# A router and expert kernel: the first 17 expert tiles wait for the rows of three groups instead of four, and VectorE's work around group 0 and the bias table stands elsewhere

## What is computed

```python
a = jax.nn.softmax(e, axis=-1)                   # 32 keys around each token
v = jnp.einsum('bts,bsf->btf', a, x)
...
probs = jax.nn.softmax(xt @ Wr + br, axis=-1)
top_p, top_idx = jax.lax.top_k(probs, TOP_K)
weights = top_p / top_p.sum(axis=-1, keepdims=True)
xe = xn[None, :, :] * ln_g[:, None, :] + ln_b[:, None, :]
h = jax.nn.gelu(jnp.einsum('end,edh->enh', xe, W1) + b1[:, None, :], approximate=False)
y = jnp.einsum('enh,ehd->end', h, W2) + b2[:, None, :]
out = (weights[:, :, None] * sel).sum(axis=1)    # sel: the rows of y of the two chosen experts
```

## Time and profile before

| | before |
|---|---|
| median of three runs | 971.86 us (970.84 to 972.05) |
| the profiled execution | 972.06 us, span 970.2 us |
| mean granted TensorE clock | 0.940 |
| TensorE, VectorE busy | 811.6 us (84%), 722.1 us (74%) |
| ScalarE, GpSimd busy | 618.1 us (64%), 608.7 us (63%) |
| routing stage | about 696 to 808 us |
| tile stream | about 811 to 936 us |

### The profile page before, as it was taken

How to read it: one execution, slowest core, us unless ns; L and a number is a source line. 1 busy time by engine, 2 the same in 40 slices (tenths; PEclk the granted TensorE clock), 3 DMA queues, 4 the chain that set the end, 5 groups by cost and what they waited for, 6 DMA issues and landing times. The chain is left out here.

```text
span 970.2 us, 25223 instructions
## 1 busy us (share of the span) xinstructions
PE 811.6 (84%) x8069; PEld 506.3 (52%) x8069; DVE 722.1 (74%) x1846; ACT 618.1 (64%) x1384; POOL 608.7 (63%) x758
## 2 busy tenths in 40 slices
PE   2888999999999999999999989847677746999950
PEld 2455555555555555555555544411355524999940
DVE  4586888888888888888888853669788651777747
ACT  4577777777878777787777832248534503888830
POOL 1127887878878788787888839810007772666650
PEclk8899999999999999999999999967999867999985
DMA  7007999994000000000000033032001111333327
GB/s 235 1 2 148 157 207 158 65 6 2 0 0 0 0 0 0 0 0 0 0 0 0 0 90 87 0 104 90 3 4 54 49 53 53 83 90 92 93 67 237
DMA packets 105406, 54.10 MB, mean 56 GB/s; under 512 B 42624, under 2 KB 96664, under 8 KB 105360
## 3 DMA queue, kind: packets, MB, share of 16 engines
q1 hardware_dynamic: 98976, 43.34, 28.9%
q0 software_dynamic: 4544, 9.38, 3.0%
q10 hardware_dynamic: 1840, 0.79, 0.4%
HBM read 21.49 MB, written 29.44 MB: 52 GB/s over the span
## 5 line engine op out<-in xcount | busy, mean ns | idle before, releaser
L398 POOL TENSOR_TENSOR s_w<-s_xsh,s_w_mem 128x512 f32<-128x512 f32 x186 | 251.8, 1354 | 8.9 <-DVE s_w_mem L570 3.4
L570 DVE SCALAR_TENSOR_TENSOR s_w_mem<-s_w_mem,s_eta,lp_g 128x256 f32<-128x256 f32 x496 | 217.8, 475 | 24.0 <-PE lp_g L733 18.6
L495 ACT ACTIVATE s_xsh<-s_w,l_keep_lr 128x256 f32<-128x256 f32 x384 | 173.8, 505 | 17.5 <-POOL l_keep_lr L418 17.4
L1484 POOL DMA_INDIRECT f_yg<-f_yr,f_xmeta x78 | 78.4, 1005 | 54.5 <-DVE f_yr L1823 41.7
L1479 POOL DMA_INDIRECT f_xg<-f_xrow,f_place x64 | 64.0, 999 | 48.0 <-DVE f_place L1719 28.8
L403 POOL TENSOR_TENSOR s_xsh<-s_w,l_keep 128x512 f32<-128x512 f32 x64 | 72.1, 1126 | 0.0
L1459 ACT ACTIVATE f_hh<-fp_v,f_bcol 128x256 f32<-128x256 f32 x156 | 61.1, 476 | 13.1 <-DVE f_hs_lo L1814 5.6
L489 ACT COPY l_wt<-lp_b 128x512 f32<-128x512 f32 x96 | 56.4, 588 | 15.0 <-PE lp_b L719 15.0
L719 PE MATMUL lp_b<-s_cst,s_w 128*128 128x128 f32 x384 | 61.7, 284 | 0.0
L1588 PE MATMUL fp_v<-f_xf,s_w_hi 128*128 128x256 bf16 x312 | 55.3, 279 | 1.6 <-DVE f_xmeta L1803 1.2
L707 PE MATMUL lp_h<-s_w,l_gf 128*32 128x128 f32 x1024 | 41.2, 278 | 18.3 <-ACT l_gf L482 18.3
(11 more groups left out here) (345 smaller groups left out, 2036.1 us busy)
## 6 DMA issues: line engine op xcount, KB each, us to landing
f_xg<-s_pad SPq DMA_DIRECT2D x1, 17280.0 KB, 107.5
f_xt<-f_xg SPq DMA_DIRECT2D x39, 130.0 KB
r_w<-in_L_ffn_W_dram SPq DMA_DIRECT2D x16, 256.0 KB, 3.1
s_w<-f_yg SPq DMA_DIRECT2D x16, 256.0 KB, 3.9
...
```

Source lines behind the costliest of these rows:

```text
L398: nc.gpsimd.tensor_tensor(W[k][:, half(h), :], KW[k][:, half(h), :], M[k][:, half(h), :], ALU.add).then_inc(w_ready[k], 1)
L495: m = nc.scalar.mul(KW[k][:, b, :], W[k][:, b, :], keep_lr[:, b:b + 1])
L570: i = nc.vector.scalar_tensor_tensor(out=M[k][:, b, :], in0=M[k][:, b, :], scalar=eta[:, b:b + 1], in1=ps_g[b][:, 0:256], op0=ALU.mult, op ...
L1484: nc.gpsimd.indirect_dma_start(sb["yg"][:, :], bass.IndirectOffsetOnAxis(ap=xmeta[:, j, a, 0:1].bitcast(mybir.dt.int32), axis=0), yr[j % R ...
```

## The change

Tiles that are full from the first three groups alone come first. After group 2, `carry_a` holds `carry` less 255, so `tiles_a` counts only full tiles of each expert; together they are at least `NA` = (2 x 128 x 8 x 3 - 8 x 255 + 255) // 256 = 17 jobs, and `ends_a` is cut off at 17. The first 17 jobs take their owner and start from that table, the other 22 from what is left. The scatters of the last group count in a semaphore of their own, `sent_last`, for which SP waits ahead of the 18th load. The number of jobs, their work and their result rows' places stay.

Around it: the mask of a block is one instruction for four batches instead of four; the end of the late softmax (its sum, reciprocal and product) and the masks of blocks 2 and 3 stand behind group 0's `normed` on VectorE, and blocks 2 and 3 behind `router(0)` and `counts(0)` on TensorE; the eight `bias` steps are spread over the four `routed(g)`, one ahead of the logits and one behind the choice; of the 76 unused matmuls behind `ps_o` 36 stand ahead of it and 20 behind it, and `ps_o` waits for `mine` only.

```diff
     GT = NT // GR
+
+    NA = (2 * 128 * GT * (GR - 1) - E * (SL - 1) + SL - 1) // SL
...
+        sent, sent_last = sem("f_sent"), sem("f_sentl")
...
-                sp.wait_ge(owner_ready, 3)
-                sp.wait_ge(sent, 16 * 2 * NT)
+                sp.wait_ge(owner_ready, 4)
+                sp.wait_ge(sent, 16 * 2 * GT * (GR - 1))
                 for j in range(NJ):
+                    if j == NA:
+                        sp.wait_ge(sent_last, 16 * 2 * GT)
...
@@ -1440,16 +1445,20 @@
                 turned_weights(0)
                 turned_weights(1)
                 for g in range(GR):
-                    if 2 * g + 2 < NTB:
+                    if g >= 1 and 2 * g + 2 < NTB:
                         turned_weights(2 * g + 2)
                     roots(g)
                     rows(g)
                     features(g)
-                    if 2 * g + 3 < NTB:
+                    if g == 0:
+                        turned_weights(2)
+                    elif 2 * g + 3 < NTB:
                         turned_weights(2 * g + 3)
                     second(g)
                     odds(g)
-                act.wait_ge(owner_ready, 4)
+                    if g == 0:
+                        turned_weights(3)
+                act.wait_ge(owner_ready, 5)
...
-                                                         row[k][:, tile_of(g, i), :], None).then_inc(sent, 16)
+                                                         row[k][:, tile_of(g, i), :], None).then_inc(sent if g < GR - 1 else sent_last, 16)
...
@@ -1542,14 +1551,20 @@
                 for g in range(GR):
                     if g >= 1:
                         unused(nc, sb, ps_am, 16)
-                    if 2 * g + 2 < NTB:
+                    if g >= 1 and 2 * g + 2 < NTB:
                         weights(2 * g + 2)
                         values(2 * g + 2)
                     router(g)
-                    if 2 * g + 3 < NTB:
+                    if g == 0:
+                        weights(2)
+                        values(2)
+                    elif 2 * g + 3 < NTB:
                         weights(2 * g + 3)
                         values(2 * g + 3)
                     counts(g)
+                    if g == 0:
+                        weights(3)
+                        values(3)
...
-                pe.wait_ge(owner_ready, 3)
+                unused(nc, sb, ps_am, 36)
+                pe.wait_ge(owner_ready, 2)
                 pe.wait_ge(tab, E + 8)
                 for h in range(NH):
                     m = nc.tensor.matmul(ps_o[:, h, :], btab[:, 128 * h:128 * h + 128], mine[:, :], start=True, stop=True)
                 m.then_inc(table_done, 1)
-                unused(nc, sb, ps_am, 76)
+                unused(nc, sb, ps_am, 20)
...
                 def masked(n):
...
-                    for b in range(B):
-                        nc.vector.tensor_tensor(am[n % 2][:, b, :].rearrange("p (r j) -> p r j", j=WIN),
-                                                e[:, n, b:b + 1, :].to_broadcast([128, 4, WIN]), band, ALU.mult)
+                    nc.vector.tensor_tensor(am[n % 2][:, :, :].rearrange("p b (r j) -> p b r j", j=WIN),
+                                            e[:, n, :, :].rearrange("p b (a j) -> p b a j", a=1).to_broadcast([128, B, 4, WIN]),
+                                            band.rearrange("p (a r) j -> p a r j", a=1).to_broadcast([128, B, 4, WIN]), ALU.mult)
...
+                def bias_piece(i):
+                    if i >= 1:
+                        dve.wait_ge(tab, E + i)
+                    bias(i).then_inc(tab, 1)
+
+                def routed(g, meanwhile=lambda: None):
+                    bias_piece(2 * g)
...
                     nc.vector.tensor_tensor(both[:, :, :].rearrange("p e n -> p n e"), one[:, :, :], two[:, :, :], ALU.add).then_inc(count_ready, 1)
+                    bias_piece(2 * g + 1)
+                    meanwhile()
                     dve.wait_ge(ex_ready, g + 1)
...
                 link(nc.vector.tensor_copy(carry[:, :], lim[:, :, 0]))
+                link(nc.vector.memset(ends_a[:, 0:1], 0.0))
...
                 nc.vector.tensor_tensor(er, er, bc, ALU.subtract).then_inc(soft, 1)
+                valued(0)
                 dve.wait_ge(sb["exp_ready"], 2)
                 nc.vector.tensor_reduce(m_late, er, AX.X, ALU.add).then_inc(soft, 1)
-                valued(0)
+                valued(1)
+                spread(0)
+                normed(0)
                 dve.wait_ge(soft, 10)
                 nc.vector.reciprocal(m_late, m_late).then_inc(soft, 1)
                 dve.wait_ge(soft, 11)
                 nc.vector.tensor_tensor(er, er, bc, ALU.mult).then_inc(soft, 1)
+                remainder(0)
                 dve.wait_ge(soft, 12)
                 masked(2)
-                valued(1)
-                for g in range(GR):
+                routed(0, lambda: masked(3))
+                valued(2)
+                masked(4)
+                valued(3)
+                for g in range(1, GR):
...
+                    if g == GR - 2:
+                        link(nc.vector.tensor_scalar(carry_a[:, :], carry[:, :], float(1 - SL), None, ALU.add))
                     if 2 * g + 3 < NTB:
                         valued(2 * g + 3)
 
-                link(nc.vector.tensor_tensor(over[:, :, :], carry[:, :].rearrange("p (e a) -> p e a", a=1).to_broadcast([128, E, 16]), lim[:, :, :], ALU.is_gt))
-                link(nc.vector.tensor_reduce(tiles[:, :], over[:, :, :], AX.X, ALU.add))
-                link(nc.vector.tensor_scalar(tiles[:, :], tiles[:, :], float(SL), None, ALU.mult))
+                def filled(c, d):
+
+                    link(nc.vector.tensor_tensor(over[:, :, :], c.rearrange("p (e a) -> p e a", a=1).to_broadcast([128, E, 16]), lim[:, :, :], ALU.is_gt))
+                    link(nc.vector.tensor_reduce(d[:, :], over[:, :, :], AX.X, ALU.add))
+                    link(nc.vector.tensor_scalar(d[:, :], d[:, :], float(SL), None, ALU.mult))
...
+                def beyond(a, z, ends_of):
+                    link(nc.vector.tensor_tensor(past[:, a:z, :], job[:, 0:z - a].rearrange("p (j a) -> p j a", a=1).to_broadcast([128, z - a, E - 1]),
+                                                 ends_of.rearrange("p (a e) -> p a e", a=1).to_broadcast([128, z - a, E - 1]), ALU.is_ge))
...
+                def gaps(a, z, gap):
+                    link(nc.vector.tensor_tensor(past[:, a:z, :], past[:, a:z, :],
+                                                 gap[:, :].rearrange("p (a e) -> p a e", a=1).to_broadcast([128, z - a, E - 1]), ALU.mult))
+
+                filled(carry_a[:, :], tiles_a)
+                link(nc.vector.tensor_tensor_scan(ends_a[:, 1:E + 1], ones[:, 0:E], tiles_a[:, :], 0.0, ALU.mult, ALU.add))
+                link(nc.vector.tensor_scalar(ends_a[:, 1:E + 1], ends_a[:, 1:E + 1], float(SL * NA), None, ALU.min))
+                link(nc.vector.tensor_tensor(tiles_a[:, :], ends_a[:, 1:E + 1], ends_a[:, 0:E], ALU.subtract))
+                filled(carry[:, :], tiles)
+                link(nc.vector.tensor_tensor(tiles[:, :], tiles[:, :], tiles_a[:, :], ALU.subtract))
                 link(nc.vector.tensor_tensor_scan(ends[:, :], ones[:, 0:E], tiles[:, :], 0.0, ALU.mult, ALU.add))
-                link(nc.vector.tensor_tensor(past[:, :, :], job[:, :].rearrange("p (j a) -> p j a", a=1).to_broadcast([128, NJ, E - 1]),
-                                             ends[:, 0:E - 1].rearrange("p (a e) -> p a e", a=1).to_broadcast([128, NJ, E - 1]), ALU.is_ge))
+                beyond(0, NA, ends_a[:, 1:E])
+                beyond(NA, NJ, ends[:, 0:E - 1])
                 link(nc.vector.tensor_reduce(owner[:, :], past[:, :, :], AX.X, ALU.add))
                 nc.vector.tensor_copy(owner_i[:, :], owner[:, :]).then_inc(owner_ready, 1)
                 nc.vector.tensor_scalar(mine[:, :], owner[:, :], cst[:, C_ROW:C_ROW + 1], None, ALU.is_equal).then_inc(owner_ready, 1)
...
+                link(nc.vector.tensor_scalar(gap_a[:, :], tiles_a[:, 0:E - 1], -1.0, float(REGION), ALU.mult, ALU.add))
+                link(nc.vector.tensor_tensor(gap_b[:, :], gap_a[:, :], tiles[:, 0:E - 1], ALU.subtract))
+                link(nc.vector.tensor_tensor(gap_b[:, :], gap_b[:, :], tiles_a[:, 1:E], ALU.add))
+                gaps(0, NA, gap_a)
+                gaps(NA, NJ, gap_b)
...
-                part = lambda i: cst[0:NSPLIT, C_PART + i:C_PART + i + 1]
...
+                link(nc.vector.tensor_scalar(owner[:, NA:NJ], owner[:, NA:NJ], tiles_a[:, 0:1], None, ALU.add))
+                nc.vector.tensor_tensor(start_i[:, 0:NA], owner[:, 0:NA], job[:, 0:NA], ALU.add).then_inc(owner_ready, 1)
+                nc.vector.tensor_tensor(start_i[:, NA:NJ], owner[:, NA:NJ], job[:, 0:NJ - NA], ALU.add).then_inc(owner_ready, 1)
                 dve.wait_ge(table_done, 2 * GR + 1)
                 nc.vector.tensor_copy(bcol[:, :, :], ps_o).then_inc(owner_ready, 1)
```

43 lines of the change are left out of this document (18 added, 25 removed).

## The result

The changed kernel takes 960.01 us in the median of five runs (955.34 to 962.06), the kernel before 971.86 (970.84 to 978.14) beside it: a ratio of 0.9854 (95% interval 0.9819 to 0.9888), faster by 11.9 us (at least 1.1%, by the interval's upper end). The prediction was 951.3 (947.5 to 955.5): the direction is right, some two fifths of the predicted gain are missing.

A forecast was written before the change was run, and what follows sets the result against it. The first load's issue was taken to bound the kernel, now set by the tile table (start_i, 789.9) rather than the 48th scatter. 972.06 - 19.95 (earlier load) - 0.8 (full clock at the head) = 951.3 us, range 947.5 to 955.5.

The forecast's parts named there:

- The bound and the mechanism: First load to end: 159.3 us follow the first load's issue and move with it; the load goes 19.95 us earlier.
- 3.83 + 2.75: VectorE's table, from carry to start_i: 3.83 us as before plus 2.75 us for the new table's added operations.
- No hole in TensorE near the fourth tile: Stream: group 3's late scatters leave yr covered by about 1 us; a hole there would prove GpSimd falls behind.
- 20.75: Whole gain in us: 19.95 from the earlier first load and 0.8 from full clock at the stream's head.
- the 0.8 us: Stream's head: short idle keeps TensorE at full clock for the first turn and products, 0.8 us, bounds 0 to 1.0.
- bound one: Groups 0 to 2: the 48th scatter, which the first load waits for, starts at 786.3 to 787.0, lands 788.5 to 789.2.
- TensorE's logits come at 713.2 (716.31 - 3.1): Group 0's router: logits come 3.1 us earlier, as xn does, so GpSimd starts at 722.65.
- Rival 1: Table or stream's head late: half-clock spells in group 2 or 3, start 1 to 4 us later, 953 to 956; 15%.
- rival 3: Stream: GpSimd falls behind, scatters beside VectorE's copies take longer, yr not free in time, 955 to 965 us; 9%.
- 6 us at full clock: Ahead of ps_o on TensorE: 36 unused matmuls take 6 us at full clock, 11.5 if all at half.
- GpSimd makes up 0.35 us a tile: Under the stream: a pair of result scatters takes 2.61 us in a tile of 2.96, recovering 0.35 us each.
- Cost: nothing: Under the stream: group 3's scatters beside the first tiles send the first result 1.5 to 2 us late, at no cost.

The follow-up runs named there:

- warm0: The changed kernel with 25 unused matmuls instead of 5 ahead of group 0's turns alone: 954.72 us, ratio 0.9781 to the kernel before.
- warm: The changed kernel with 25 unused matmuls ahead of group 0's turns and 35 ahead of group 3's, instead of 5 each: 954.51 us, ratio 0.9772.
- warm3: The changed kernel with 35 unused matmuls instead of 5 ahead of group 3's turns alone: 961.02 us, ratio 0.9845.
- tuned_head: warm with 4 instead of 16 unused matmuls in group 1, the last bias piece earlier, and 36 instead of 20 behind ps_o: 952.06 us, ratio 0.9772.
- again: The changed kernel once more with nothing edited, for a second profile and more times: 961.68 us, ratio 0.9864.
- after: The changed kernel as first measured and profiled, against the kernel before: 960.01 us, ratio 0.9854.

## Why the prediction was half right

**Right.** The bound and the mechanism: 17 tiles start under group 3's scatters, and all that follows the first load moves with it (129.5 against 129.6 us). `xn` at 706.89 for 707.0. `start_i` and not the scatter releases SP. From `carry` (787.20) to the last `start_i` (793.82) it takes 6.6 us, for 3.83 + 2.75 predicted. No hole in TensorE near the fourth tile. With TensorE kept busy the predicted chain comes out: first scatter 26.45 us behind the mark in warm0 and 27.16 in warm for 26.46, the first load in warm 94.3 for 94.8. That warm's gain is 975.16 - 954.51 = 20.7 us for 20.75 is luck in part, since its first products ran at half clock (0.61) and the 0.8 us of that sum isn't in it.

**The step that failed** is in bound one: "TensorE's logits come at 713.2 (716.31 - 3.1)". It carried the old distance from `xn` to the logits over to the earlier `xn`, and with it a full clock. They came at 715.26. The change moves mask 2, its turn and `values(2)` behind the router, and the prediction never worked out what TensorE does from 705.3 to 709.1 instead: nothing, for 3.76 us, and 13 us at half clock or near it follow. The counts came late too, and the first scatter 3.3 us after its time. Rival 1 had the mechanism and its size (each spell 1 to 2 us for VectorE, 953 to 956), but looked for it in groups 2 and 3, with 15%; the range ended at 955.5. The median, 960.01, lies among rival 3's 955 to 965, but its hole in TensorE did not come. Full clock in group 0 alone, by 20 more unused matmuls, brings the ratio to 0.9781. The Trainium skill, "TensorE: Matmul & The Clock Gate", Part 1, says that an idle array falls to the half rate, and the trace agrees (0.50 behind those 3.76 us); the prediction used it for the stream's head only. Its 36 unused matmuls "6 us at full clock" took 6.01, though 15.03 / 76, which it names for them, would give 7.1.

Group 3's half clock (5.99 us idle, logits 3.42) is the second part: `carry` ended at 787.37 for 783.3 predicted, after a 17th scatter that was 2.4 to 3.1 late already, and `start_i` 4.1 us late for 789.9, which is the whole miss of the first load (795.06 for 790.95). The spell itself was there before (logits 1.94 in one profile, 3.42 in the other); the prediction carried over the quick one. In the median it isn't told from nothing (warm3, and warm against warm0).

**The 0.8 us at the stream's head** did not come: the idle time ahead of the first turn was short, 0.47 us, and the turn ran at full clock, but the products behind it, from 799, in a stretch with a granted clock of 0.57. What it would have been worth stays open: in tuned_head a full clock brought 0.56 us up to the third tile, which then lost more at half clock.

**"GpSimd makes up 0.35 us a tile"** was wrong, "Cost: nothing" right. A pair took 0.96 + 1.40 + 0.60 = 2.96 us, exactly the tile's pace, once GpSimd was late enough to start each second scatter 0.73 us into the subtractions instead of 0.48; the earlier trace rows's 1.004 held only where it waited for `yr`. `again` happened to start in time, kept 1.006, and was no faster for it.

**The rest of the miss.** The profiled execution of after, 955.34, is the fastest of its five; against before's 972.06 it gains 16.7 of the 20.75. The median lies 4.7 higher. In `again` 4.1 us stand ahead of the mark, in code that the change doesn't touch, and 3.9 of them already ahead of 641 us, where the attention stage begins (GpSimd's last L937 starts at 640.81, in after at 636.91). A spell at half clock stands there as well:

```profile
623.88 1.11 PE L1048 MATMUL rp_t<-s_cst,s_xl 128*128 128x128 f32 x4 [2.85 <-DVE s_xl L1076]
```

In after the same turns start at 621.52, behind 1.55 us idle, and take 0.66; the granted clock from 618 to 632 us is 1.00 there and 0.90 and 0.85 in `again`. Why the wait is longer in one execution than in another, whether such a spell stands behind the other executions near 960, and whether it is more frequent in the changed kernel, stays open.
